# A two-block transformer layer in float32: the context split made in two pieces, and the rows of maxima cleared by GpSimd instead of by SyncE's transfers

## The reference, cut to what matters

```
h1 = ln(x);  x = attn(h1, h1) @ o1 + x           # self-attention, 20 heads of 16
h2 = ln(x);  x = attn(h2, context) @ o2 + x      # cross-attention, 361 keys
h3 = ln(x);  a, g = split(h3 @ ff_w1 + ff_b1)
out = (a * gelu(g)) @ ff_w2 + ff_b2 + x
```

## Time and profile before

| | us |
|---|---|
| median of 3 runs | 1356.31 |
| lowest, highest | 1354.94, 1356.92 |
| the profiled execution, its own time | 1353.86 |
| its span, first to last instruction | 1352.1 |
| PE busy in the span | 1300.3 (96%) |
| POOL busy in the span | 382.7 (28%) |
| mean granted TensorE clock | 0.991 of full |

### The profile page before, as it was taken

How to read it: one execution, slowest core, us unless ns; L and a number is a source line. 1 busy time by engine, 2 the same in 40 slices (tenths; PEclk the granted TensorE clock), 3 DMA queues, 4 the chain that set the end, 5 groups by cost and what they waited for, 6 DMA issues and landing times. The chain is left out here.

```text
span 1352.1 us, 35354 instructions
## 1 busy us (share of the span) xinstructions
PE 1300.3 (96%) x13364; PEld 1206.1 (89%) x13364; DVE 825.6 (61%) x1729; ACT 682.4 (50%) x1558; POOL 382.7 (28%) x545
## 2 busy tenths in 40 slices
PE   6999889999999999999999999999889999999999
PEld 4999778899898889889898898898689999999999
DVE  5554377777777777777777777777664324252521
ACT  5665246565565565565565565565454231313131
POOL 5421212212212212212212212212266233333331
PEclk9999799999999999999999999999999999999999
DMA  4776645445445455445445445443202101010000
GB/s 126 237 251 210 196 130 153 125 135 155 126 132 165 135 148 168 147 146 163 151 127 144 141 124 146 143 126 106 53 24 73 49 2 49 0 48 0 24 1 25
DMA packets 121670, 155.60 MB, mean 115 GB/s; under 512 B 25013, under 2 KB 115373, under 8 KB 121517
## 3 DMA queue, kind: packets, MB, share of 16 engines
q1 hardware_dynamic: 121516, 153.52, 37.4%
HBM read 62.98 MB, written 28.93 MB: 68 GB/s over the span
## 5 line engine op out<-in xcount | busy, mean ns | idle before, releaser
L1396 ACT ACTIVATE probs<-expin 120x400 f32<-120x400 f32 (+2 forms) x635 | 312.2, 505 | 158.9 <-PE expin L751 102.9
L1073 DVE TENSOR_REDUCE neg_max<-score 100x2 f32<-100x722 f32 x320 | 290.2, 907 | 58.5 <-PE score L725 46.2
L751 PE MATMUL expin<-qs,ks 128*120 128x200 f32 (+2 forms) x1270 | 235.3, 276 | 7.1 <-DMA qs<-max_parts 4.8
L751 PEld LDWEIGHTS expin<-qs,ks 128*120 128x120 f32 (+2 forms) x1270 | 191.9, 180 | 26.4 <-DMA qs<-max_parts 9.2
L725 PE MATMUL score<-ks,qs 128*100 128x362 f32 x640 | 165.2, 339 | 6.6 <-DVE neg_max L1073 4.7
L2566 DVE SCALAR_TENSOR_TENSOR hidden<-ps_a,b_cols,gelu 128x320 f32<-128x320 f32 x100 | 55.1, 551 | 163.7 <-PE ps_a L2490 159.2
L1576 POOL TENSOR_TENSOR var_eps<-mv,eps 100x1 f32<-100x1 f32 x32 | 6.1, 190 | 419.4 <-DVE mv L1141 419.4
L2728 POOL TENSOR_TENSOR hid_lo<-hidden,hid_hi 128x320 fp32r<-128x320 f32 x100 | 89.1, 892 | 120.6 <-ACT hid_hi L2636 120.4
L2648 ACT ACTIVATE gelu<-ps_g,b_cols 128x320 f32<-128x320 f32 x100 | 52.8, 528 | 134.4 <-PE ps_g L2490 134.4
L167 DVE TENSOR_REDUCE neg_max<-score 100x10 f32<-100x1000 f32 x62 | 74.4, 1200 | 57.7 <-PE score L160 57.7
L725 PEld LDWEIGHTS score<-ks,qs 128*100 128x100 f32 x640 | 82.9, 166 | 18.0 <-DVE neg_max L1073 6.3
(11 more groups left out here) (219 smaller groups left out, 2975.1 us busy)
## 6 DMA issues: line engine op xcount, KB each, us to landing
ks<-kc_parts SPq DMA_DIRECT2D x192, 181.0 KB, 3.0
qk_dram<-qk_parts SPq DMA_DIRECT2D x32, 500.0 KB, 5.3
qs<-q_parts SPq DMA_DIRECT2D x192, 75.0 KB
ks<-qk_dram SPq DMA_DIRECT2D x96, 125.0 KB
ctx_raw<-in_ctxT SPq DMA_DIRECT2D x64, 180.5 KB
ks<-kc_parts SPq DMA_DIRECT2D x96, 90.5 KB, 2.2
qs<-qk_dram SPq DMA_DIRECT2D x64, 125.0 KB
v_dram<-v_rows SPq DMA_DIRECT2D x32, 132.8 KB
```

Source lines behind the costliest of these rows:

```text
L751: mm = pe.matmul(dst, ks[a][u][:, c, j0:j0 + n], qs[a][u][:, :, q_slot(c) if a == 2 else c, :], start=True, stop=True)
L1073: ins = nc.vector.tensor_reduce(dst, src, AX_X, ALU.max, negate=True)
L1396: nc.scalar.activation(probs[e % NPT][0:n, :], expin[e % 2][0:n, 0:HG * N], ACT.Exp, scale=SCALE)\
```

## The change

In the loop, the two rows are no longer cleared by SP. GpSimd sets each of them to zero with a memory set on one partition (2000 elements for the self stack, 2400 for the cross stack), waits for it, and adds the same 16 to the same semaphore. SP's `clear_max` stays for self stacks 0 to 3 and cross stacks 0 and 1. The self stack of `c + 2` is cleared at the head of POOL's period, the cross stack of `c` at its end, behind `split_context(f)`. The split is made in two pieces of columns, 0 to 239 and 240 to 361; the first waits for `KC` 2, `VC` 0 and `VC` 1 of the sequence before, the second for its `VC` 2.

```diff
-def load_own(sp, b, qk1_dram, v1_dram, qs, ks, vs, zeros, landed):
-    clear_max(sp, qs, zeros, landed)
+def load_own(sp, b, qk1_dram, v1_dram, qs, ks, vs, landed):
...
+                if b < 4:
+                    clear_max(sp, qs[1][u], zeros, qkv1_landed[u])
+                load_own(sp, b, qk1_dram, v1_dram, qs[1][u], ks[1][u], vs[u], qkv1_landed[u])
...
-                clear_max(sp, qs[2][u], zeros, q2_landed[u])
+                if b < 2:
+                    clear_max(sp, qs[2][u], zeros, q2_landed[u])
...
+            def clear_rows(stack, landed):
+                for r in (0, 64):
+                    row = stack[r:r + 1].rearrange("p a c n -> p (a c n)").bitcast(F32)
+                    link(nc.gpsimd.memset(row, 0.0))
+                pool.sem_inc(landed, 16)
+            def clear_own(b):
+                if b is None:
+                    return
+                pool.wait_ge(pv_made, PV_AT[1, b - 2, G - 1] + 1)
+                clear_rows(qs[1][b % 2], qkv1_landed[b % 2])
+            def clear_cross(b):
+                e = EXP_AT[2, b - 2, G - 1, 2]
+                pool.wait_ge(exp_full[e % 2], e // 2 + 1)
+                clear_rows(qs[2][b % 2], q2_landed[b % 2])
...
+            def split_part(j):
+                hi, lo, raw = ctx_hi[:, :, j], ctx_lo[:, :, j], ctx_raw[:, :, j]
+                link(nc.gpsimd.tensor_tensor(hi, raw, one[:].unsqueeze(2).broadcast_to(list(raw.shape)), ALU.mult))
+                return nc.gpsimd.tensor_tensor(lo, raw, hi.bitcast(F32), ALU.subtract)
             def split_context(b):
                 pool.wait_ge(ctx_landed, 32 * (b + 1))
-                if b:
-                    pool.wait_ge(*filled(("VC", b - 1, 2)))
-                    pool.wait_ge(*filled(("KC", b - 1, 2)))
-                link(nc.gpsimd.tensor_tensor(ctx_hi[:], ctx_raw[:], one[:].unsqueeze(2).broadcast_to([P, 2, JP]),
-                                             ALU.mult))
-                nc.gpsimd.tensor_tensor(ctx_lo[:], ctx_raw[:], ctx_hi[:].bitcast(F32), ALU.subtract)\
-                    .then_inc(ctx_split, 1)
+                pool.wait_ge(*filled(("KC", b - 1, 2)))
+                pool.wait_ge(*filled(("VC", b - 1, 0)))
+                pool.wait_ge(*filled(("VC", b - 1, 1)))
+                link(split_part(slice(0, JT[2][0])))
+                pool.wait_ge(*filled(("VC", b - 1, 2)))
+                split_part(slice(JT[2][0], JP)).then_inc(ctx_split, 1)
...
             def run_out():
                 inverse_deviation(31)
                 second_residual(31)
+                clear_cross(31)
...
                 x, s, c, f = roles(p)
+                clear_own(p + 4 if p + 4 < B else None)
                 inverse_deviation(c)
                 first_residual(f)
                 second_residual(c)
                 split_context(f)
+                clear_cross(c)
```

More of the change, by code:

```diff
@@ L475, in load_qkv1 @@
                         sp.wait_ge(v_stored[i], 16 * B // NB)
-                load_own(sp, b, qk1_dram, v1_dram, qs[1][u], ks[1][u], vs[u], zeros, qkv1_landed[u])
+                if b < 4:
+                    clear_max(sp, qs[1][u], zeros, qkv1_landed[u])
+                load_own(sp, b, qk1_dram, v1_dram, qs[1][u], ks[1][u], vs[u], qkv1_landed[u])
             def cross_stack_free(b, g):
@@ L1790, in _ @@
                     sp.wait_ge(v_stored[1], 16)
-                    load_own(sp, 1, qk1_dram, v1_dram, qs[1][1], ks[1][1], vs[1], zeros, qkv1_landed[1])
+                    clear_max(sp, qs[1][1], zeros, qkv1_landed[1])
+                    load_own(sp, 1, qk1_dram, v1_dram, qs[1][1], ks[1][1], vs[1], qkv1_landed[1])
                 elif k == NK - 2:
@@ L1806, in _ @@
                     sp.wait_ge(v_stored[0], 16)
-                    load_own(sp, 0, qk1_dram, v1_dram, qs[1][0], ks[1][0], vs[0], zeros, qkv1_landed[0])
+                    clear_max(sp, qs[1][0], zeros, qkv1_landed[0])
+                    load_own(sp, 0, qk1_dram, v1_dram, qs[1][0], ks[1][0], vs[0], qkv1_landed[0])
             sp.wait_ge(landed["o_b"], 32)
```

## The result

The changed kernel takes 1340.61 us in the median of 4 runs against 1355.62 us before, a ratio of 0.9886 with a 95% interval of 0.9857 to 0.9916. One of the four runs, 1373.37 us at a mean clock of 0.892, is left out of that ratio. The forecast was 1342.2 us. Measured again (e4), the changed kernel took 1341.41 us against 1356.97 us, ratio 0.9896 (0.9872 to 0.992).

What follows compares the result with a forecast made beforehand. PE, busy 96% of the span, bounds the kernel, so only its idle time in the loop can be gained. 9.8 + 3.7 + 0.6 = 14.1 us off the median of 1356.31 gives 1342.2 us, range 1338.5 to 1351.5.

Steps and rivals of the forecast that it cites:

- The two waits: PE's idle time before `KC` 0, 9.8 us in all, and before first exponents waiting for stored maxima, 9.2 us.
- a wait recorded as "issue": PE's stall before `KC` 0, read from the timeline as waiting for POOL's `ctx_lo`: 28 times, 9.8 us.
- Split in two pieces: Term for POOL's work between `VC` 2 and `KC` 0: gain 28 x 0.35 = 9.8 us, at least 0.
- second self score: PE's L160, 1.1 us behind `KC` 0, needs DVE's maximum: fits with 0.1 us to spare, nothing charged.
- SP's cross clear: Term for SP's queue: maxima issued 0.62 us earlier, gain 3.7 us at the exponent, 0.6 us in the run-out.
- POOL's clears: Terms for POOL's self sets, about 1.8 us each, and cross sets, 2.10 us each: cost 0.
- C: Rival at the first cross score: sets take 2.59 us each, clearing is a little late, 1350.9 us; chance 0.07.
- D: Rival at PE's cross scores: one-partition sets take 2.8 us or more each, slower than before, to 1380 us; chance 0.05.
- E: Rival: the 0.35 us come back in another chain, no effect, within 2.7 us of 1356.3; chance 0.05.
- room of 0.7 us: Time to spare between the end of POOL's cross sets, 421.2, and the first cross score, 421.88 without the stall.
- VectorE beside POOL: DVE's L1148 waits for POOL, 0.45 us seen; the new sets don't meet it, cost 0.
- B: Rival at the stored maxima: landing hangs on transfer engines, not SP's issue; gain 4.1 us, 1352.2 us; chance 0.13.

Runs made afterwards that it cites:

- e4: The changed kernel measured and profiled once more, nothing changed: 1341.41 us, ratio 0.9896 to the kernel before.
- e5: Changed kernel with SP clearing the cross stacks again, GpSimd only the self stacks: 1351.31 us, ratio 0.9983 to the kernel before.
- e6: Changed kernel with SP clearing the self stacks again, GpSimd only the cross stacks: 1337.40 us, ratio 0.9886 to the kernel before.
- e3: Changed kernel with the split in one piece again and the cross clear ahead of it: 1349.63 us, ratio 0.9945 to the kernel before.
- e2: Changed kernel with the split in one piece again, clears kept on GpSimd in their places: 1370.52 us, ratio 1.0096 to the kernel before.
- e7: Changed kernel with one more GpSimd set of 1250 elements ahead of each cross clear in the loop: 1354.06 us, ratio 1.0003 to the kernel before.
- e10: Changed kernel with self clears back on SP and GpSimd's cross clear ahead of the two-piece split: 1336.73 us, ratio 0.9862 to the kernel before.
- e11: Changed kernel with the high row of the cross maxima stored by a ScalarE transfer: 1340.61 us, ratio 0.9874 to the kernel before.
- e12: Changed kernel with the edits of e10 and e11 together: 1341.67 us, ratio 0.9885 to the kernel before.
- e9: The kernel before, nothing changed, measured and profiled once more: 1356.51 us.
- e8: Changed kernel with the cross clear ahead of the two-piece split: 1340.00 us, ratio 0.9892 to the kernel before.
- e1: Changed kernel with all clears back on SP, so only the split in two pieces: 1353.97 us, ratio 0.9983 to the kernel before.

## Why the prediction was right

*What bounds it.* The two waits it named were the ones that moved. The reading of a wait recorded as "issue" by its neighbours on the timeline held: with the split in two pieces it is gone from the list.

*Split in two pieces.* Forecast: POOL pieces of 0.99, 1.24, 0.59 and 0.72 us; measured 0.99, 1.23, 0.59 and 0.72. The gain was sized at 9.8 us from the idle time of the weight loads and came to 10.5 us, since `KC` 0 moved by 0.38 us and not 0.35 us. The nearness of the second self score cost nothing: it comes 1.04 us behind `KC` 0, without a wait. One reading was loose: a third of the columns stays between `VC` 2 and `KC` 0, but by the prediction's own pieces 1.39 of 3.24 us, which is more than a third of the work; the sum doesn't use it.

*SP's cross clear.* Forecast 3.7 us at the exponent, measured 3.5 us. In the run-out it is 0.9 us instead of 0.6: the wait of 0.82 us at the earlier trace rows is gone whole. e5 and e6 show that this transfer and not the self one does it. The working took 7.0 us for the lateness before; it was 6.4 us in that profile and 8.9 us in the other, and between the two second profiles the term is 6.0 us (8.9 and 2.9). So the method was right in kind, and the agreement to 0.2 us is luck. The prediction took SP's lateness from a usual period, where, as it says, SP does no harm; the late periods it saw as two single ones. In the first profile of before, 16 of the 28 periods are late by more than 0.08 us. In 9 of them (3.4 us of lateness) the exponent follows the issue by 1.37 us, and the maxima are issued 2.3 to 2.9 us behind `MT2` instead of 1.78, because the six query transfers ahead took SP 4.0 to 4.9 us instead of 3.75. Those ahead of the maxima at 470.94:

```profile
465.93 4.90 SPq L507 DMA_DIRECT2D qs<-q_parts  x6
```

In the other 7 (2.9 us) SP issues on time and the landing is slow. After the change the two kinds are 3 periods with 0.7 us and 3 with 1.6 us. So the cleared slot is room that SP needs in its long periods. What makes the six transfers long there is open.

What the prediction left out is that the two terms are not additive. Alone, the split gives 2.3 us and the clears of e3 7.3 us (by the ratio 7.5), about 10 together, where the two give 14 to 15. The prediction had this coupling within its term (0.62 - 0.35 us of relief), but said nowhere what either part is worth alone.

*POOL's clears.* Forecast 2.10 us for a row of 2400 elements, measured 2.09 us on one partition (1.76 us for 2000). So rivals C and D fall for this kernel; their place was real all the same, as e2 (13 us slower) and e7 (even) show. E falls with the loop's 14.0 us. The room of 0.7 us was right. With the clears behind the split, it exists only because the split's second piece is short.

*VectorE beside POOL.* The subtraction and scaling at L1150 has the same spread as at the earlier trace rows, 493 ns at least and 946 ns in the median, and none of its 32 overlaps a new set. The prediction read 0.45 us as what it is held up by. The rows say more: in all 32 cases it ends 0.21 to 0.22 us behind the end of a POOL instruction that was running when it started, the shortest case included. So at the earlier trace rows some 0.7 us of the 0.94 are waiting. VectorE's maxima and subtractions did run beside the new sets, and took what they take alone (911 and 911 ns for the cross maxima, 1200 and 1199 ns for the self maxima, 250 and 250 ns for the subtraction). VectorE's busy time is 825.6 us in both profiles. By the Trainium skill's rule of the shared port pair, held for a whole instruction ("SBUF — State Buffer", on two separate sides), with which these 32 cases agree, the new sets would have had to overlap L1150 to cost anything there; no trace here has such an overlap.

*B* (landing hangs on the transfer engines) is refuted for the 9 late periods in which the landing took its usual 1.37 us: SP issued 0.65 us earlier and their lateness nearly went (3.4 to 0.7 us). Of the 7 periods with a slow landing it holds in part. In the period at 439 us the maxima were issued by 441.83 us and the exponent came at 444.62 us, 2.8 us later instead of 1.36 us, as long as in the same period of before (2.6 us); in e6, e10, e11 and e12 this period has no lateness at all. What holds up these landings is open; no run tests it.

*The total* agrees to 1.6 us (1342.2 and 1340.61), and between the profiles to 0.2 us (14.1 and 13.9), with two errors that offset each other: 1.0 us lost ahead of the 28 periods, which is within the scatter that e9 shows, and 0.8 us more gained in the loop and run-out together (14.9 against 14.1 us). That the sum is met to 0.2 us is luck; that two waits shrink, and by about how much, is not.

## What to carry to other kernels

When two waits of an engine stand one behind the other in a loop, cutting the first only brings the engine sooner to the second; cost the second anew with that shift, and shorten both chains. Work moved off a queue that is late goes to an idle engine at no cost only up to the wait that it now precedes: measure that room before the move (here 0.7 us of a 4.3 us job), and where the order allows it, put the moved work ahead of the critical work and not behind it. A wait of 1 us was followed by a fall of the clock once here and cost 2.7 us in all (e8), so a rare long wait can be worth more than its length.

## What the runs showed of the hardware

GpSimd's memory set takes as long on one partition as on 128: 2094 ns for 1x2400 and 2104 ns for 128x2400, 1760 and 1763 ns for 2000 elements. Each transfer of the cross maxima (9.4 KB) costs the issuing engine about 0.8 us: 0.83 us on SyncE (1.66 us for two) and 0.77 us in the median on ScalarE (e11). From the end of the issue to the start of a PE that waits for them it is 1.37 us in most cases, and up to 2.9 us in single periods (e4, e9). The clock's loss is placed differently in each execution of the same loop: in the first period (27.8 us at 0.88 in e9, 24.9 us at 1.00 in the changed kernel's first profile), in the last 20 us of the run-out (0.84 or 1.00), and within the 28 periods in e5 and e8 alone. In e10 three runs at a mean clock of 0.993 to 0.994 took 1336.1 to 1336.7 us, and one at 0.987 took 1342.6 us, so the clock separates these. It isn't all that separates runs of one kernel: two runs of e1 at 0.992 took 1349.09 and 1355.52 us. An instruction of VectorE that scales and shifts 100x384 float32 (L1148 before, L1150 after) waited in all 32 cases, before and after, for the end of a GpSimd instruction that was running when it started, and ended 0.21 to 0.22 us behind that.
